# Feed-forward stage of a fused attention block on one core: order of its ScalarE and VectorE lists changed, last tile sent in halves

## The reference

```python
x = x + _L0_xattn_ref(_layernorm(x, axis=-1), ctx_2048, ctx_2048, mask_BxS2_ff1, ...)
x = x + _L0_ffn_ref(_layernorm(x, axis=-1), L0_ffn_w_gate, L0_ffn_w_up, L0_ffn_w_down, L0_ffn_subln_weight)
```

```python
def activation_quant(x):
    scale = 127.0 / jnp.clip(jnp.max(jnp.abs(x), axis=-1, keepdims=True), EPS, None)
    return jnp.clip(jnp.round(x * scale), -128.0, 127.0) / scale
...
gate = bit_linear(x, w_gate)
up = bit_linear(x, w_up)
activated = up * jnp.square(jax.nn.relu(gate))
activated = subln(activated, subln_weight)
return bit_linear(activated, w_down)
```

## Time and profile before

| what | value |
|---|---|
| median of three runs | 485.03 us |
| the profiled execution's own time | 485.14 us |
| its span, first to last instruction | 483.0 us |
| PE busy | 422.2 us (87%) |
| DVE busy | 378.6 us (78%) |
| ACT busy | 331.4 us (69%) |
| POOL busy | 147.7 us (31%) |
| granted TensorE clock, mean | 0.958 of full |
| first feed-forward matmul | 268.80 us |

### The profile page before, as it was taken

How to read it: one execution, slowest core, us unless ns; L and a number is a source line. 1 busy time by engine, 2 the same in 40 slices (tenths; PEclk the granted TensorE clock), 3 DMA queues, 4 the chain that set the end, 5 groups by cost and what they waited for, 6 DMA issues and landing times. The chain is left out here.

```text
span 483.0 us, 8260 instructions
## 1 busy us (share of the span) xinstructions
PE 422.2 (87%) x2816; PEld 212.9 (44%) x2816; DVE 378.6 (78%) x821; ACT 331.4 (69%) x474; POOL 147.7 (31%) x146
## 2 busy tenths in 40 slices
PE   4989899997999989999859987988979888999954
PEld 1346446563454654546535432432424333434321
DVE  3587687799989989999898577787877878777761
ACT  5398997594766948668659477765757677878740
POOL 1119100091006410022000345345444545554520
PEclk9998999999999999999959997998998999999988
DMA  8999990004032320321214322233323334434223
GB/s 215 308 393 386 352 353 38 1 2 175 16 118 88 130 87 0 113 104 45 78 56 152 99 45 36 63 76 76 77 44 83 71 76 77 98 83 72 67 58 94
DMA packets 58993, 54.38 MB, mean 113 GB/s; under 512 B 45200, under 2 KB 45200, under 8 KB 58832
## 3 DMA queue, kind: packets, MB, share of 16 engines
q1 hardware_dynamic: 58064, 50.55, 35.7%
q0 software_dynamic: 896, 3.41, 1.9%
HBM read 39.27 MB, written 4.19 MB: 90 GB/s over the span
## 5 line engine op out<-in xcount | busy, mean ns | idle before, releaser
L1207 PE MATMUL ps<-tern,xqT 128*128 128x512 bf16 x512 | 121.7, 389 | 23.0 <-ACT relu L1050 12.7
L1039 POOL TENSOR_TENSOR actg<-acts,subln 128x512 f32<-128x512 f32 x64 | 87.1, 1372 | 99.6 <-DVE acts L1118 94.8
L1207 PEld LDWEIGHTS ps<-tern,xqT 128*128 128x128 bf16 x512 | 48.3, 99 | 93.0 <-issue 23.1
L1217 PE MATMUL ps<-tern,aqT 128*128 128x512 bf16 x256 | 63.1, 403 | 8.6 <-DMA aqT<-aq 8.6
L1061 ACT ACTIVATE square<-acts 128x2048 bf16<-128x2048 f32 x16 | 30.6, 1911 | 47.4 <-DVE acts L1118 47.4
L1123 DVE TENSOR_REDUCE amax<-actg 128x1 f32<-128x1024 f32 x32 | 38.9, 1217 | 27.6 <-POOL actg L1039 27.6
L1118 DVE TENSOR_TENSOR acts<-relu,ps 128x512 f32<-128x512 f32 x64 | 43.5, 681 | 5.1 <-ACT relu L1054 4.0
L1217 PEld LDWEIGHTS ps<-tern,aqT 128*128 128x128 bf16 x256 | 26.3, 104 | 44.2 <-DMA aqT<-aq 9.6
L1054 ACT ACTIVATE relu<-relu 128x512 f32<-128x512 f32 x64 | 40.3, 630 | 2.0
L536 DVE SCALAR_TENSOR_TENSOR fl<-ps,fh 128x512 f16<-128x512 f32 x64 | 39.6, 682 | 2.4 <-ACT fh L399 2.4
L1050 ACT ACTIVATE relu<-ps 128x512 f32<-128x512 f32 x64 | 37.0, 579 | 5.5 <-PE ps L1207 5.5
(11 more groups left out here) (162 smaller groups left out, 957.9 us busy)
## 6 DMA issues: line engine op xcount, KB each, us to landing
tern<-in_wffn SPq DMA_DIRECT2D x24, 512.0 KB, 11.8
wst<-in_wffn SPq DMA_DIRECT2D x24, 512.0 KB, 3.3
xs<-in_x SPq DMA_DIRECT2D x4, 1024.0 KB, 7.2
out<-res SPq DMA_DIRECT2D x16, 256.0 KB, 2.2
ctxf<-in_ctxT POOLq DMA_DIRECT2D x3, 1024.0 KB, 10.0
xno<-in_wkT SPq DMA_DIRECT2D x4, 256.0 KB, 5.4
ctxf<-in_ctxT SPq DMA_DIRECT2D x4, 256.0 KB, 6.1
fh<-in_wvT SPq DMA_DIRECT2D x1, 1024.0 KB, 7.8
```

The costliest lines, as they stand in the source:

```text
L1039: nc.gpsimd.tensor_tensor(actg[:, s % 2, q], acts[:, s % 2, q], subln[:, q], ALU.mult)\
L1207: mm = nc.tensor.matmul(acc, xqT[:, s % XT, k, :], weights[k][:, 512 * c:512 * c + 512], start=(k == 0), stop=(k == KC - 1))
L1217: mm = nc.tensor.matmul(down_bank(s), aqT[:, s % 2, k, :], down_w[:, k, :], start=(k == 0), stop=(k == FK - 1))
```

## The change

Six things change, all in ffn and SecondLN. The computation is the same.

1. ScalarE: quarter(s, 0) goes ahead of squares(s - 1) and root(s - 1), and quarter(s, 2) ahead of scaled(s - 1).
2. VectorE: multiply(s, 0) goes ahead of quantiser(s - 1); multiply(s, 2) ahead of whole(s - 1), and result_scales between them; multiply(s, 3) ahead of largest(s, 0).
3. The last group's layer norm statistics (four tiles, three instructions each) go from one tile in each of steps 1 to 4 to two instructions in each of steps 1 to 6, between result(s - 3) and multiply(s, 1), without a drain for each tile. Its later parts go from steps 5, 6, 7, 8 and 9 to steps 7, 8, 9, 10 and 10.
4. scaled(15) and whole(15), each one instruction over 2048 columns, become two over 1024.
5. The aqT transposition of tile 15 becomes two of half size, each waiting for its half of whole(15); the first of them also keeps the wait for the down product.
6. down(15) waits for the first half before its first matmul and for the second before its ninth.

```diff
@@ -41,7 +41,8 @@
 CPM = NCH // 3
 KVW = 2 * HD + 2
 XT = 3
-ROOT2_AT, SCALE2_AT, QUANTISE2_AT, CUBES2_AT = 5, 6, (7, 8), 9
+STATS2_AT = range(1, 7)
+LARGEST2_AT, SCALE2_AT, QUANTISE2_AT, CUBES2_AT = 7, 8, (9, 10), 10
 QUAD = P // HD
 
 W_SCALE = 16.0
@@ -895,6 +896,14 @@
         nc.vector.tensor_reduce(self.ends[:, 0, t:t + 1], tile, AX_X, ALU.max)
         nc.vector.tensor_reduce(self.ends[:, 1, t:t + 1], tile, AX_X, ALU.min)
 
+    def statistic(self, nc, g, t, j):
+
+        tile = self.xs[:, g * GT + t, :]
+        if j == 0:
+            nc.vector.bn_stats(self.stats[:, t, :], tile)
+        else:
+            nc.vector.tensor_reduce(self.ends[:, j - 1, t:t + 1], tile, AX_X, (ALU.max, ALU.min)[j - 1])
+
     def largest(self, nc, dve, link):
 
         ends, mean = self.ends, self.means[:, :, 0]
@@ -973,6 +982,7 @@
         scaled_ok, aq_ok = sem("scaled_ok"), sem("aq_ok")
         D_filled, res_ok = sem("D_filled"), sem("res_ok")
         aqT_in = [sem(f"aqT_in_{k}") for k in range(2)]
+        last_aqT_in = [sem(f"last_aqT_in_{h}") for h in range(2)]
         out_done = [sem(f"out_done_{k}") for k in range(2)]
         chain = sem("ffn_chain")
 
@@ -1011,7 +1021,14 @@
                     if j >= XT:
                         sp.wait_ge(U_filled, NB * (j - XT + 1))
                     sp.dma_start_transpose(xqT[:, j % XT], xqb[:, j % 2, :]).then_inc(xqT_in[j % XT], 16)
-                if 1 <= s <= NT:
+                if s == NT:
+                    sp.wait_ge(D_filled, s - 2)
+                    for h in range(2):
+                        sp.wait_ge(aq_ok, s + h)
+                        sp.dma_start_transpose(aqT[:, (s - 1) % 2, FK // 2 * h:FK // 2 * h + FK // 2],
+                                               aq[:, (s - 1) % 2, HALF * h:HALF * h + HALF])\
+                            .then_inc(last_aqT_in[h], 16)
+                elif 1 <= s < NT:
                     sp.wait_ge(aq_ok, s)
                     if s >= 3:
                         sp.wait_ge(D_filled, s - 2)
@@ -1072,22 +1089,26 @@
             def scaled(s):
 
                 act.wait_ge(qs_ok, s + 1)
-                nc.scalar.activation(actg[:, s % 2, :], actg[:, s % 2, :], ACT.Identity, bias=magic_up[:, :],
-                                     scale=qs[:, s:s + 1]).then_inc(scaled_ok, 1)
+                width = FF if s < NT - 1 else HALF
+                for at in range(0, FF, width):
+                    part = actg[:, s % 2, at:at + width]
+                    nc.scalar.activation(part, part, ACT.Identity, bias=magic_up[:, :], scale=qs[:, s:s + 1])\
+                        .then_inc(scaled_ok, 1)
 
             for s in range(NT + 1):
+                if s < NT:
+                    quarter(s, 0)
                 if s > 0:
                     squares(s - 1)
                     root(s - 1)
                 if s < NT:
-                    quarter(s, 0)
                     quarter(s, 1)
+                    quarter(s, 2)
                 if s > 0:
                     scaled(s - 1)
                 if s < NT:
-                    quarter(s, 2)
                     quarter(s, 3)
-                if s == ROOT2_AT:
+                if s == LARGEST2_AT:
                     act.wait_ge(ln2.var_ok, G)
                     nc.scalar.activation(ln2.sd[:, :], ln2.var[:, :], ACT.Sqrt).then_inc(ln2.sd_ok, 1)
 
@@ -1147,11 +1168,14 @@
 
             def whole(s):
 
-                dve.wait_ge(scaled_ok, s + 1)
                 if s > 1:
                     dve.wait_ge(aqT_in[s % 2], landed(s - 2, 2))
-                nc.vector.tensor_scalar(aq[:, s % 2, :], actg[:, s % 2, :], ROUND, None, ALU.subtract)\
-                    .then_inc(aq_ok, 1)
+                width = FF if s < NT - 1 else HALF
+                for h in range(FF // width):
+                    dve.wait_ge(scaled_ok, s + h + 1)
+                    part = slice(width * h, width * h + width)
+                    nc.vector.tensor_scalar(aq[:, s % 2, part], actg[:, s % 2, part], ROUND, None, ALU.subtract)\
+                        .then_inc(aq_ok, 1)
 
             def result(s):
 
@@ -1161,27 +1185,12 @@
                 nc.vector.scalar_tensor_tensor(out=res[:, s % 2, :], in0=down_bank(s), scalar=dq[:, s:s + 1],
                                                in1=xs[:, s, :], op0=ALU.mult, op1=ALU.add).then_inc(res_ok, 1)
 
-            for s in range(NT + 3):
-                if 1 <= s <= NT:
-                    quantiser(s - 1)
-                if s == NT:
-                    whole(s - 1)
-                if s >= 3:
-                    result(s - 3)
-                if s < NT:
-                    multiply(s, 0)
-                if s in range(2, NT + 1, 2):
-                    result_scales(slice(s - 2, s))
-                if s < NT:
-                    multiply(s, 1)
-                if 1 <= s < NT:
-                    whole(s - 1)
-                if s < NT:
-                    multiply(s, 2)
-                    largest(s, 0)
-                if 1 <= s <= GT:
-                    ln2.statistics(nc, dve, 0, G - 1, s - 1)
-                if s == GT + 1:
+            def last_group(s):
+
+                if s in STATS2_AT:
+                    for n in (2 * STATS2_AT.index(s), 2 * STATS2_AT.index(s) + 1):
+                        ln2.statistic(nc, G - 1, *divmod(n, 3))
+                if s == LARGEST2_AT:
                     ln2.largest(nc, dve, link)
                 if s == SCALE2_AT:
                     ln2.scale(nc, dve, link, 0, G - 1)
@@ -1190,8 +1199,28 @@
                     ln2.quantise(nc, link, 0, G - 1, (half, half + 1))
                 if s == CUBES2_AT:
                     cubes(slice(NT - GT, NT))
+
+            dve.drain()
+            for s in range(NT + 3):
+                if s < NT:
+                    multiply(s, 0)
+                if 1 <= s <= NT:
+                    quantiser(s - 1)
+                if s == NT:
+                    whole(s - 1)
+                if s >= 3:
+                    result(s - 3)
+                last_group(s)
+                if s < NT:
+                    multiply(s, 1)
+                    multiply(s, 2)
+                if s in range(2, NT + 1, 2):
+                    result_scales(slice(s - 2, s))
+                if 1 <= s < NT:
+                    whole(s - 1)
                 if s < NT:
                     multiply(s, 3)
+                    largest(s, 0)
             link.end()
 
         @block.tensor
@@ -1210,10 +1239,13 @@
 
             def down(s):
 
-                pe.wait_ge(aqT_in[s % 2], landed(s, 2))
+                if s < NT - 1:
+                    pe.wait_ge(aqT_in[s % 2], landed(s, 2))
                 if s >= 2:
                     pe.wait_ge(res_ok, s - 1)
                 for k in range(FK):
+                    if s == NT - 1 and k % (FK // 2) == 0:
+                        pe.wait_ge(last_aqT_in[k // (FK // 2)], 16)
                     mm = nc.tensor.matmul(down_bank(s), aqT[:, s % 2, k, :], down_w[:, k, :],
                                           start=(k == 0), stop=(k == FK - 1))
                 mm.then_inc(D_filled, 1)
```

## The result

The changed kernel takes **456.64 us** (median of 4 runs, 453.92 to 457.34) against 484.78 for the kernel before in the same session. The ratio of the two means is 0.9397, with a 95% interval of 0.9343 to 0.945. The forecast was 455.6 in a range of 449 to 467. The profiled execution took 456.15 us, with a span of 454.0 and a mean granted clock of 0.977, against 485.14, 483.0 and 0.958 before.

The account below looks back on a forecast made before the run. TensorE's own work was taken as the least time, with a ring across engines causing its waits. From 485.14, 33.3 earlier plus 1.6 in the tail less 5.4 of waits is 29.5 saved: 455.6 us, range 449 to 467.

Parts of the forecast that it names:

- The ring: Per feed-forward step: squares, quarters 1 and 2, scaled, whole, multiply 3 now take 8.60 us, under TensorE's 10.42.
- the forecast's main term: Feed-forward at TensorE's own pace: step 15 starts at 418.2, last sum of squares at 428.8, 33.3 us earlier.
- TensorE's waits: Steps 1 to 10: VectorE needs 106.8 us against TensorE's 100.7; lag 6.1 less 0.7 makes 5.4 us.
- The term for the two engines' meeting: VectorE waiting for GpSimd's instruction under way, before result_scales or whole: 0.75 us per step, between 0 and 2.48.
- the later parts of the layer norm: VectorE's layer norm work moved to steps 7 to 10: taken at 1.19 us per step, like the statistics.
- the slack: Even layer norm steps: aqT lands at 16.7, the down product wants it at 17.4, so VectorE may lag 0.7 us.
- Rival A: VectorE waits for both GpSimd instructions in layer norm steps: 9.2 us more, 464.8 us; chance 0.2.
- Rival B: VectorE and GpSimd hardly meet; VectorE at 19.85 per two steps, TensorE never waits: 450.2 us; chance 0.2.
- C: Another latency, late landings or 11.35 us per step, keeps the late tiles' old pace: 463 to 468 us; chance 0.08.
- D: Later whole and aqT make each down product wait 2 us or more, dropping TensorE to half clock: 505 us; chance 0.02.
- From step 15 to the last squares: Path from TensorE's start of the last tile through its quarters to the last sum of squares: 10.6 us.
- The tail: Last tile in halves: 0.3 us from scaled and whole, 1.4 from earlier transposition; 1.7, rounded to 1.6, bounds 0 and 2.3.

Follow-up runs that it names:

- largest first: Changed kernel with one VectorE swap undone, largest(s,0) again ahead of multiply(s,3): 472.55 us, 0.9664 to 0.9769 of the kernel before.
- quarter 0 behind: Changed kernel with one ScalarE swap undone, quarter(s,0) after squares(s-1) and root(s-1): 489.70 us, 1.0074 to 1.0164 of the kernel before.
- multiply 0 behind: Changed kernel with one VectorE swap undone, multiply(s,0) after quantiser(s-1) and result(s-3): 471.74 us, 0.971 to 0.9791 of the kernel before.
- layer norm bunched: Changed kernel with one layer norm tile and drain in each of steps 1 to 4, later parts in steps 5 to 9: 457.54 us.

## Why the prediction was right, step by step

**The ring, and the forecast's main term: shown.** TensorE's start of step 15 was put 149.4 + 5.4 = 154.8 after the first matmul and came 424.54 - 268.55 = 155.99 after it. The forecast's ring needs quarter 0 ahead of the squares and multiply 0 ahead of the quantiser; undoing either gave 220.06 and 200.74 in place of 185.45. The squares late in the stage are 10.36 apart on average (395.69 to 426.77), where 10.4 to 10.5 was said. One sign of being right did not come: ScalarE still waits for VectorE, 12.2 us in front of the squares, and largest 0.7 for GpSimd. No wait of TensorE goes back to it, but the forecast had the squares follow TensorE's pace while in the even steps they follow multiply 3, at the end of VectorE's late list.

**TensorE's waits, 5.4 forecast, 7.4 measured.** The gaps are 6.15 (5.00 for aqT, 1.15 for banks), and each of the nine costs 0.16 more, since a gate and up row lasts 7.07 but what follows starts 6.91 behind its start where nothing is between; that would make 7.6, and the difference of start times below gives 7.4. TensorE's own work, 15 x 6.91 + 13 x 3.46 = 148.6, is 0.8 less than the 149.4 of the forecast and hides part of that: 155.99 - 148.6 = 7.4. The mechanism is the one written down: a VectorE with slightly more work than TensorE for two steps. From multiply 3 to multiply 3 over two steps:

```profile
319.40 0.68 DVE L1139 TENSOR_TENSOR acts<-relu,ps 128x512 f32<-128x512 f32 x1
...
326.99 1.75 DVE L1177 TENSOR_SCALAR aq<-actg 128x2048 bf16<-128x2048 f32 x1
...
341.01 0.68 DVE L1139 TENSOR_TENSOR acts<-relu,ps 128x512 f32<-128x512 f32 x1
...
363.30 0.68 DVE L1139 TENSOR_TENSOR acts<-relu,ps 128x512 f32<-128x512 f32 x1
```

From 319.40 to 341.01 that is 21.61 against the 21.35 that I had added up. The term for the two engines' meeting, taken at 0.75 per step between 0 and 2.48, measures (21.61 - 19.85) / 2 = 0.88. A second term was too small, the later parts of the layer norm: I took them "at the same 1.19", and they take 1.12, 1.88, 1.03 and 1.96 in steps 7 to 10, so the pair of steps up to 363.30 takes 22.29 and the next, up to 385.56, 22.26. Against these two, the slack was wider than 0.7: the ten steps took 109.7 (multiply 3 of step 0 starts at 275.87), and less 100.7 and 0.7 that would be 8.3 of waits, not 7.4. The small rest is three waits for a bank, which I had put at nothing "until VectorE is almost 2 us late": the multiplies 3 of steps 1, 8 and 10 were, by up to 0.59 beyond that. The experiment with largest first shows how thin that cover is.

**Rival A, both GpSimd instructions waited for: did not happen.** Whole takes 1.60 to 1.75 in the odd steps 3 to 9 and 2.30 in step 1, where it started (284.27) as GpSimd's second instruction did (its two take 2.50 from 282.98), not the 2.5 to 3.5 that would have shown A, and in the even step each of the two tiny instructions waited for one GpSimd instruction (0.85 and 1.20), with VectorE getting in between the two. The Trainium skill, SBUF — State Buffer, "Who interferes with whom", says that between a GpSimd instruction and a VectorE instruction of the kinds that the prediction names the first to issue has the port for its whole length and the other waits; these rows agree, with waits of one instruction and no more, and the row at 106.95 in the earlier trace rows stays the exception. **Rival B, that the two hardly meet, did not happen either:** 12.5 us of VectorE's time hang on the length of GpSimd's instructions alone. When they are halved the kernel lands near B's number, 449.98 against 450.2, though that is partly chance, since B's sum has the forecast's tail in it.

**Rivals C and D: no.** The transpositions of tile rows (the two halves are in this line, at its lower end), answering to the earlier trace rows:

```profile
DMA to landing us min/median/max: 3.2/4.3/4.4
```

None was late in this profile; in nine of the eleven experiments the slowest landed 5.2 to 6.0 after its issue. The 10.36 per step excludes the 11.35 of C, and the longest wait for aqT ahead of the tail is 0.99, half of the 2 that D needs at every tile.

**From step 15 to the last squares: 10.6 forecast, 11.38 measured** (424.54 to 435.92). I followed quarter 3 and took multiply 3 to be free when it came. In fact it stood behind whole(14), which took 1.66 beside GpSimd, with scaled ahead of it 0.2 late. This is the same meeting of the two engines, which I had costed in the layer norm steps and forgotten in the last one.

**The tail: 1.6 forecast, 2.86 measured, and here the sizes were off.** The changed kernel's tail:

```profile
435.92 1.91 ACT L1078 ACTIVATE square<-acts 128x2048 bf16<-128x2048 f32 x1 [1.25 <-DVE acts L1139]
...
440.77 0.69 DVE L1177 TENSOR_SCALAR aq<-actg 128x1024 bf16<-128x1024 f32 x1 [1.38 <-ACT actg L1095]
...
442.44 0.74 DVE L1185 SCALAR_TENSOR_TENSOR res<-ps,dq,xs 128x512 f32<-128x512 f32 x1
...
443.21 0.33 SPq L1017 DMA_DIRECT2D out<-res  x1
443.63 2.66 SPq L1028 DMA_TRANSPOSE aqT<-aq  x2
```

Squares to issue is 7.71 against 7.96 in the earlier trace rows (0.25 for the 0.3). Issue to TensorE's start is 443.63 to 447.11, 3.48 against 4.44: 0.96 for the 1.4, as a half transposition lands 3.2 after its issue at best, where I took 3.0 by size. The last product takes 3.61 at full clock against 5.22: 1.61 that I had put at nothing, having assumed that it would start at half clock. This is the largest miss of the tail. The rows show that the clock fell in the gap ahead of down(14) and that it had risen again by the end of it; the experiment without halves shows the last product at full clock behind a gap of 3.44 too. The first half stood ready at 441.46 and was issued at 443.63, behind the output, as forecast; the experiment with the output moved gave the 2.14 back.

**The reckoning.** The attention ended 0.25 earlier, step 15 came 1.2 later than forecast (waits 2.0 more, own work 0.8 less), the path to the squares 0.8 later, the tail 1.3 earlier. Together 0.5 late: a span of 454.0 for a forecast of 453.5; the median of the runs is 1.0 above the forecast. The closeness is in part luck, since the misses cancel. Of the 28.75 in the profiles the halves hold 1.4 and the spread layer norm about 2; if the parts add up, the other 25 are the two orders together, of which neither alone gives any.

**Still open.** Why 2.15, 2.63 and 3.44 of gap leave the next product at full clock and 1.98, 2.42, 2.55 and 2.61 don't (below) wasn't settled. No run moves multiply 2 and quarter 2 alone; their share is known only from the 11.6 between two experiments, both with quarter 0 behind the squares. Nor was the rest of the feed-forward part of largest first and multiply 0 behind attributed row by row: the waits for banks carry it, the split between them and the tail is read from the trace and not tested alone.

## What to carry to other kernels

When several engines run written-out lists, follow the ring through all of them and ask at each swap which instruction on another engine must move with it: here one engine's new order alone was worth 0 us, the other's -17, and both together 28. Put an instruction that frees a PSUM bank ahead of anything of its engine that nobody is waiting for, and put runs of tiny VectorE instructions where GpSimd is idle, not behind the instruction that starts it. On a queue, look at what each finished transfer stands behind: an output that nobody waits for held the last transposition for 2.1 us.

## What the hardware showed that I had not expected

- A VectorE instruction on two columns, 0.15 to 0.17 us alone, lasts up to 1.20 beside GpSimd's products of about 1.25, and the one on a single column (0.22) up to 0.52. The tiny ones lose 0.70 and 1.03, and whole, on 2048 columns (1.23), loses 0.5 in the odd steps: in these rows the cost of meeting GpSimd goes by the number of VectorE's instructions that meet it and the moment, not by their size.
- The length of a gap did not tell the clock behind it. The sixteen matmuls of the last product took 3.61 to 3.63 behind gaps of 1.03 (layer norm bunched), 2.15 (changed), 2.63 (multiply 0 behind) and 3.44 (last tile whole), and 5.04 to 5.30, the first of them at half clock, behind gaps of 1.98 (ScalarE's order of before), 2.42 (largest first), 2.55 (quarter 0 behind), 2.61 (VectorE's order of before) and 5.10.
- A transposition of half the columns lands 3.2 after its issue at best, not in half of the 4.3 of a whole one. With the 2.4 of xqT's 512 columns, four times the columns take 1.8 times as long.
